# One tile of gathered node rows per round: from SyncE's single-row DMAs to a GpSimd gather

## What is computed

```python
h_nodes = mlp2(x, node_W1, node_b1, node_W2, node_b2)
h_edges = mlp2(edge_attr, edge_W1, edge_b1, edge_W2, edge_b2)
msg_in = concatenate([h_nodes[dst], h_nodes[src], h_edges], axis=-1)
msgs = mlp2(msg_in, msg_W1, msg_b1, msg_W2, msg_b2)
agg = segment_sum(msgs, dst) / maximum(counts, 1)
out = x + mlp2(concatenate([x, agg], axis=-1), upd_W1, ...)
out = layernorm(out) * ln_g + ln_b
return layernorm(x + out)
```

## Time and profile before

| | |
|---|---|
| median of 3 runs | 4963.27 us (4941.1 to 4977.42) |
| span of the profiled execution | 3612.0 us |
| the profiled execution's own time | not listed apart from its span |
| PE, PEld busy | 2874.1 us (80%), 2219.4 us (61%) |
| DVE, ACT busy | 2737.3 us (76%), 2994.3 us (83%) |
| POOL busy | 2674.4 us (74%) |
| instructions | 103943 |
| TensorE clock granted, mean | 0.748 |
| HBM traffic | 330.78 MB read, 13.01 MB written, 95 GB/s |

### The profile page before, as it was taken

One profiled execution on the slowest core, in us unless ns is written; L12 is line 12 of the kernel. 1 busy time (PEld: TensorE's weight loads), 2 busy tenths in 40 slices (PEclk: granted clock), 3 DMA queues, 4 the chain that ended last, 5 costly groups with the idle time before them and its releaser, 6 DMA issues.

```text
span 3612.0 us, 103943 instructions
## 1 busy us (share of the span) xinstructions
PE 2874.1 (80%) x16224; PEld 2219.4 (61%) x16224; DVE 2737.3 (76%) x20847; ACT 2994.3 (83%) x23073; POOL 2674.4 (74%) x2823
## 2 busy tenths in 40 slices
PE   4878888877878878888778888777778878877885
PEld 2666666666666666666666666656665656656664
DVE  4777778778777777777787777787777777877876
ACT  4998888888887888988888888888878888888785
POOL 4777777777777777777777777777777777777773
PEclk7687777677777777777777777777777776677766
DMA  7454444454444454444454444444444444444441
GB/s 225 78 113 100 87 94 100 89 102 96 95 95 86 96 102 90 101 100 88 93 103 85 102 96 95 99 95 87 98 92 99 101 89 96 90 92 102 96 95 43
DMA packets 263059, 350.77 MB, mean 97 GB/s; under 512 B 111714, under 2 KB 199121, under 8 KB 252514
## 3 DMA queue, kind: packets, MB, share of 16 engines
q1 hardware_dynamic: 169792, 246.77, 32.0%
q0 software_dynamic: 90624, 95.15, 14.5%
q10 hardware_dynamic: 1954, 2.14, 0.2%
HBM read 330.78 MB, written 13.01 MB: 95 GB/s over the span
## 4 chain that ended last, share of the span: by engine, by line
POOL 62%; issue 21%; PE 8%; DMA 4%; DVE 4%; DVEq 0%; ACT 0%; SPq 0%; ACTq 0%; POOLq 0%
POOL b_ring L834 62%; DMA b_ring<-b_table,src 4%; PE p_pre L696 2%; PE p_pre L702 1%; DVE colbuf L642 1%; PE p_sum L716 1%; PE p_hid L849 1%; DVE comb L939 1%; DMA work<-in_xT 1%; PE p_pre L705 0%; PE p_last L995 0%; PE p_last L996 0%; DVEq L627 0%; DVE stats L1032 0%; ACT colbuf L642 0%
## 5 line engine op out<-in xcount | busy, mean ns | idle before, releaser
L834 POOL DMA_INDIRECT b_ring<-b_table,src x2800 | 2652.0, 947 | 858.9 <-issue 844.8
L642 ACT COPY colbuf<-shared 64x4 uint8 x21134 | 2127.4, 190 | 159.9 <-issue 148.4
L642 DVE COPY colbuf<-shared 64x4 uint8 x17511 | 1377.6, 194 | 308.6 <-issue 301.9
L696 PE MATMUL p_pre<-wa_ring,comb 128*128 128x64 f32 x6250 | 1047.1, 329 | 0.0
L696 PEld LDWEIGHTS p_pre<-wa_ring,comb 128*128 128x128 f32 x6250 | 996.8, 245 | 0.9 <-issue 0.8
L727 ACT ACTIVATE comb<-p_hid,b_e 64x320 f32<-64x320 f32 x1250 | 652.8, 522 | 360.4 <-PE p_hid L849 350.9
L939 DVE SCALAR_TENSOR_TENSOR comb<-shared,p_const 64x640 f32<-64x640 int32 x625 | 554.0, 887 | 458.8 <-PE p_pre L696 336.2
L716 PEld LDWEIGHTS p_sum<-hot_ring,msg 128*65 128x65 f32 x6250 | 589.2, 181 | 500.0 <-DVE agg L949 265.0
L716 PE MATMUL p_sum<-hot_ring,msg 128*65 128x64 f32 x6250 | 649.5, 269 | 291.1 <-DVE agg L949 166.6
L702 PE MATMUL p_pre<-b_ring,ident 128*128 128x320 f32 (+1 forms) x1250 | 583.4, 559 | 341.4 <-DMA b_ring<-b_table,src 340.8
L849 PE MATMUL p_hid<-e_ring,w_e 128*128 128x320 f32 x1250 | 626.2, 591 | 49.0 <-DMA e_ring<-in_edgeT 40.0
(11 more groups left out here) (106 smaller groups left out, 599.2 us busy)
## 6 DMA issues: line engine op xcount, KB each, us to landing
e_ring<-in_edgeT SPq DMA_DIRECT2D x250, 320.0 KB
shared<-in_dst_row SPq DMA_DIRECT2D x125, 640.0 KB
b_ring<-b_table SPq DMA_DIRECT2D x3200, 0.2 KB
b_ring<-b_table,src POOLq DMA_INDIRECT x2800
e_ring<-in_edgeT SPq DMA_DIRECT2D x50, 400.0 KB
shared<-in_dst_row SPq DMA_DIRECT2D x25, 800.0 KB
wa_ring<-a_table SPq DMA_DIRECT2D x625, 16.0 KB
work<-in_xT SPq DMA_DIRECT2D x25, 250.0 KB
```

What stands on the lines that cost most here:

```text
L642: end = copy(colbuf[:, special % COLBUF, at:at + 1].bitcast(U8), of[j])
L696: return eng.matmul(p_pre[:, i % 2, k * H:(k + 1) * H], comb[:, i % COMBS, k * P:(k + 1) * P], wa_ring[:, i % RING, :], start=k == 0, stop ...
L834: eng.indirect_dma_start(b_ring[:, b_slot(i), k, :], None, b_table, bass.IndirectOffsetOnAxis(ap=src[:, u * TILES + k:u * TILES + k + 1], ...
```

## The change

SP fetches no single rows. The tile that it fetched in each round is gathered by POOL with the unit's other tiles, and PE waits for it by the slot's semaphore, whose count at unit 24 rises from four gathers a round to five. The list of node numbers, its place in `to_ab`, its loads, its semaphores and the input that it came from are gone. The general path counts the new gather too.

```diff
-ROW_TILE = (24, 3)
-ROWS_A_STEP = 8
-ROWS_FROM = 7
...
-    row_list = to_ab[0:1, :, :, :, :].rearrange("o s t q n -> o (s t q n)").bitcast(I32)[:, at:at + P]
-    assert at + P <= SR * 2 * 2 * GJ * H
+    assert at <= SR * 2 * 2 * GJ * H
...
-    row_list_in = sem("row_list_in")
-    row_in = [sem(f"rows{q}_in") for q in range(4)]
...
-    def by_pool(i):
-
-        return [k for k in gathered(i) if (i, k) != ROW_TILE]
-
     def b_value(r, i):
 
-        each = [16 * len(by_pool(j)) for j in range(ROUND) if b_slot(j) == b_slot(i)]
-        so_far = [16 * len(by_pool(j)) for j in range(i + 1) if b_slot(j) == b_slot(i)]
+        each = [16 * len(gathered(j)) for j in range(ROUND) if b_slot(j) == b_slot(i)]
+        so_far = [16 * len(gathered(j)) for j in range(i + 1) if b_slot(j) == b_slot(i)]
...
         load_list(eng, LEADIN, LEADIN, HALF_AT, list_in[0])
 
-        load_rows(eng, 0)
-
-    def load_rows(eng, r):
-
-        eng.dma_start(row_list, a["rows"][ds(r * P, P)].unsqueeze(0)).then_inc(row_list_in, 16)
-
-    def fetch_rows(eng, r, i):
-
-        first = (i - ROWS_FROM) * ROWS_A_STEP
-        if first == 0:
-            wait_alone(eng, row_list_in, 16 * r + 16)
-        _, nodes = nc.values_load_multi_w_load_instructions(
-            row_list[:, first:first + ROWS_A_STEP], engines=[eng.engine], min_val=0, max_val=N - 1,
-            skip_runtime_bounds_check_because="an edge's source is a node")
-        unit, tile = ROW_TILE
-        for q, node in enumerate(nodes):
-            eng.dma_start(b_ring[first + q:first + q + 1, b_slot(unit), tile, :], b_table[ds(node, 1), :])\
-               .then_inc(row_in[q % len(row_in)], 16)
-        if first + ROWS_A_STEP == P:
-            load_rows(eng, r + 1)
-
     def sync_last(eng):
 
-        eng.wait_ge(row_list_in, 16 * ROUNDS + 16)
         eng.wait_ge(list_in[0], 32 * ROUNDS + 32)
...
-            if 0 <= i - ROWS_FROM < P // ROWS_A_STEP:
-                fetch_rows(eng, r, i)
             step(k)
...
-            for k in by_pool(i):
+            for k in gathered(i):
                 eng.indirect_dma_start(b_ring[:, b_slot(i), k, :], None, b_table,
...
-            if j == ROW_TILE[0]:
-                for arrived in row_in:
-                    wait_alone(eng, arrived, (rr + 1) * (16 * P // len(row_in)))
             eng.wait_ge(b_in[b_slot(j)], b_value(rr, j))
...
-            eng.wait_ge(b_in[b_slot(u)], 16 * len(by_pool(u)))
+            eng.wait_ge(b_in[b_slot(u)], 16 * len(gathered(u)))
...
-    rows = g["src"].reshape(-1, ROUND, TILES, P)[:, ROW_TILE[0], ROW_TILE[1], :]
-    d["rows"] = np.concatenate([rows, np.zeros_like(rows[0:1])]).reshape(-1)
```

## The result

The changed kernel took **4677.55 us** (median of 4 runs, 4663.59 to 4709.13) against 4960.24 us (4941.1 to 4977.42) of the kernel before: ratio **0.9443**, 95% interval 0.9397 to 0.9489. It is 5.6% faster where 0.63% slower was forecast, and outside the range.

What follows compares the result with a forecast made beforehand. The prediction took POOL's unbroken gathers to bound the kernel: 3612.0 us span plus 31.3 for 25 gathers, nothing for SP's relief or DMA traffic, and 1351.3 us carried over unchanged, gave 4994.6 us; range 4941 to 5021 us.

Steps and rivals of the forecast that it cites:

- What bounds the kernel: Whole span: POOL's gathers run without a stop, 1.252 us each; all but about 108 us is pace times count.
- The gather on POOL: POOL's queue, one added gather a round: 25 at 1.252 us, 31.3 us more.
- lower bound of 30.1 us: Kernel's end: at most 1.2 us of the added gathers' 31.3 can be hidden before PE's last source term.
- Rival 3: Added gather, fifth in a slot's line: each as long as the longest seen, 52.0 us, giving 5015.3 us; chance 0.07.
- SP's relief: SP's queue without row fetches: some 1.6 ms of its time saved, worth nothing in the sum; 104.3 us at most.
- POOL is their cover: DVE's waits for destination rows, 104.3 us: hidden because POOL does not wait for DVE or PE, except for free slots.
- The 1351.3 us carried over: Gap between the profiled span, 3612.0 us, and the timed median, 4963.27 us: kept unchanged in the forecast.
- Rival 2: Timed runs: another engine, such as ACT, sets the pace and hides the gather; price 0, 4963.3 us; chance 0.08.
- Rival 1: Timed runs: stretched inside, POOL's pace with them; the added gathers cost 43.0 us, giving 5006.3 us; chance 0.12.
- Rival 4: Time outside the span: grows with program length, so 10026 fewer instructions save 130.3 us, giving 4864.3 us; chance 0.07.
- What would show it: Changed profile: 2825 gathers, 1.25 us interval, span 3643, SP waiting over 1 ms more; wrong if POOL waits over 1 us.

Runs made afterwards that it cites:

- j7_after: The changed kernel, no edit, in a job where the kernel before took 3630.74 us: 3655.39 us, ratio 1.0074.
- j1_full_unused: Changed kernel plus all of SP's former list loads, register loads and 3200 row fetches, into an unread spare tile; before at 3614.07 us: 3642.81 us, ratio 1.0085.
- j3_semaphore_incs: Changed kernel plus 9600 semaphore increments on SP in the 16 former fetching steps; before at 3632.43 us: 3647.66 us, ratio 1.0051.
- j2_full_unused: Changed kernel plus all of SP's former fetch work, rows into an unread spare tile; before at 4951.10 us: 4935.75 us, ratio 0.9977.
- j1_before_again: The kernel before, unchanged, profiled anew: 3614.91 us, ratio 1.0003.

## Why the prediction was wrong

**What bounds the kernel: right for the trace, wrong for the timed runs.** In the short condition POOL's pace and POOL's count give the time. In the long one they do not, and the whole working rested on this reading.

**The gather on POOL: right in kind, somewhat too large, in the short condition.** Forecast 31.3 us on 3612.0, a ratio of 1.0087. Measured 1.0074 (1.0056 to 1.0093), 24.7 us between the medians. That lies under the lower bound of 30.1 us, by less than the scatter of that job (before 3617.91 to 3635.97 us); but the six variants with 2825 gathers in the other short jobs lie under it too, 14.8 to 28.7 us above before. The bound was wrong at the end of the kernel. The 5.38 us of the earlier trace rows run from the start of a gather (3489.85 us), and the prediction added them to the end of the last one, so 2.1 us could be hidden and not 1.2. And the tail did change: from the start of the last gather to the end of the span are 3612.0 - 3567.4 = 44.6 us before and 3657.3 - 3616.9 = 40.4 in j7_after, whose last source term starts 3.5 us after that gather and not 7.5:

```profile
3620.43 1.38 PE L692 MATMUL p_pre<-b_ring,ident 128*128 128x320 f32 x2
```

Rival 3, the dear gather, did not happen: the interval is (3616.9 - 62.3) / 2824 = 1.259 us in j7_after, 0.007 above before, and 1.252 in the traces of j1_full_unused and j3_semaphore_incs.

**SP's relief is worth nothing: the step that failed.** I wrote that "they are worth nothing in the sum, because POOL is their cover" and named the whole gain if the cover is gone: 104.3 us, the wait of DVE for destination rows. In the long condition the cover is gone, and I had priced its loss from a trace in which it was whole. There the same fetches take 6 us for eight instead of 3.13, and SP's work costs 263 us, from j2_full_unused, where SP leads the chain. The trace had the warning in it, and I named it without pricing it: two `a_table` loads 5.63 us apart in steps with fetches, in a kernel whose unit takes 3504.1 / 625 = 5.6 us. SP had almost no reserve in 16 of 25 steps. Its waits in the trace of before, first in the 16 fetching steps of one round (1489.8 to 1581 us), then in the nine that follow (1581 to 1629 us):

```profile
SPq L815 <- PE p_pre L696: 0.9, 2, 0.6
```

```profile
SPq L815 <- PE p_pre L696: 28.6, 8, 7.8
```

Summed over all rounds, 39.9 of the 755.6 us follow a step with fetches.

**The 1351.3 us carried over: why the wrong cover went unseen.** "I carry it over unchanged" was the choice. It treated the 1351.3 us as time in which the kernel does nothing, when they are a second condition in which POOL no longer sets the pace. The runs have 1.8 us around the span of the changed kernel and 2.3 us around that of j1_before_again. The Trainium skill, "Runtime: NRT & Kernel Launch", section "The ~15µs preamble/postamble breakdown", puts about 15 us there and so spoke against the choice; the measured times are smaller still. I had made a rival of it with a chance of 0.12, but stretched POOL's pace with everything else. POOL's own gathers are not stretched at all (947 ns in the trace of before and in that of the changed kernel); only the time between is, and not at the median, which is 1.25 us in both traces.

**The rivals.** Rival 2 had the right form, "in the timed runs another engine sets the pace", with ACT as the engine and a price of 0; the work that cost the time was SP's. Rival 1's premise, stretched inside, was right; its price and sign were wrong. Rival 4, faster by 130.3 us through the length of the program, came nearest and had the right sign, and its cause is wrong: 9600 more instructions cost nothing.

**What would show it.** In the short condition the signs came true: 2825 gathers, "issue" before them, 2098.7 us of waiting on SP at line 783 where it was 755.6, and DVE's wait for destination rows down from 104.3 to 45.4 us with no gain for the span. In the long one SP waits 2777 us for its `a_table` slot in the changed kernel and 929 in j2_full_unused; "POOL waits for PE in places of over 1 us", named as the sign of a wrong prediction, is what the first trace after the change shows.

## What to carry to other kernels

Where the profiled span and the timed runs differ by a third, a sum made on the span need not hold for the times; here it had the wrong sign. First find out whether the gap is around the kernel or inside it, and until then let the range cover both. An engine that has waits over a whole round may have none in the steps that matter: compare its work in one step with the length of that step, and price what happens if the step's instructions take twice as long. Work on a queue should be spread until its fullest step is as full as the mean: the same 3200 fetches cost 263 us in 16 steps and 50 us in 22, in the long condition.

## What the runs showed of the hardware

In the long condition instructions of SP, ACT and DVE start late. It is clearest at the start of the main part, in ACT's timeline of the changed kernel:

```profile
83.41 0.19 ACT L632 COPY colbuf<-shared 64x4 uint8 x1 [1.91 <-issue]
84.81 0.19 ACT L632 COPY colbuf<-shared 64x4 uint8 x1 [1.20 <-issue]
86.22 0.19 ACT L632 COPY colbuf<-shared 64x4 uint8 x1 [1.22 <-issue]
87.61 0.19 ACT L632 COPY colbuf<-shared 64x4 uint8 x1 [1.20 <-issue]
```

Copies of 0.19 us that wait for nobody start 1.40, 1.41 and 1.39 us apart. DVE's copies of the same stretch lie in between, SP's DMAs beside them:

```profile
84.12 0.17 DVE L632 COPY colbuf<-shared 64x4 uint8 x1 [1.11 <-issue]
85.51 0.16 DVE L632 COPY colbuf<-shared 64x4 uint8 x1 [1.22 <-issue]
86.92 0.17 DVE L632 COPY colbuf<-shared 64x4 uint8 x1 [1.25 <-issue]
```

```profile
84.10 0.69 SPq L779 DMA_DIRECT2D shared<-in_dst_row  x1
```

So in this stretch each of the three starts one instruction in about 1.4 us, DVE half way between two of ACT's, while the copies themselves take their usual time. This is not so all the time: over the whole trace ACT is idle 451.2 us before such copies, against 159.8 us in j7_after. POOL's gathers go on at an unchanged pace in this stretch:

```profile
83.32 0.95 POOL L800 DMA_INDIRECT b_ring<-b_table,src  x1 [0.30 <-issue]
84.57 0.94 POOL L800 DMA_INDIRECT b_ring<-b_table,src  x1 [0.30 <-issue]
```

In the short condition the same copies run back to back, 34 in 3.48 us (ACT's timeline of j7_after):

```profile
79.62 3.48 ACT L632 COPY colbuf<-shared 64x4 uint8 x34 [0.56 <-issue]
```

A rival is TensorE's clock: its granted share is 0.60 to 0.62 of full speed in the long runs of the two kernels and 0.74 to 0.76 in the short ones. It does not make these late starts. In the stretch from 80 to 100 us (first the changed kernel in the long condition, then j7_after; busy us and instructions of PE, PEld, DVE, ACT, POOL, then the clock) the clock is 0.50 and 0.55, at or near the lower of its two levels (1.2 GHz) in both, PE does next to nothing in the long one, and ACT gets through 28 instructions instead of 144:

```profile
80.00:100.00 20.00, 2.50 (x4) 1.18 (x4) 3.83 (x30) 3.83 (x28) 15.13 (x17) 0.50 0.55 111
```

```profile
80.00:100.00 20.00, 10.21 (x34) 7.08 (x34) 14.49 (x136) 17.57 (x144) 15.14 (x16) 0.55 0.70 134
```

How much of the rest of the long time is PE's lower clock was not tried. What makes the two conditions was not tried either and is not known; it is common to all runs of a job and not tied to a chip.
